# Moving the second half of the agent input from VectorE to ScalarE in a recurrent kernel, and one state sum ahead of the first cell's terms

## The reference, cut to what matters

```python
encoded = tanh(xt @ We + st @ Ue + be)
new_state = tanh(einsum('bd,cds->bcs', xt, Wx) + einsum('bs,cst->bct', st, Ws) + bk)
mem = concatenate([concatenate([encoded, err[:, None]], 1)[:, None, :], mem[:, :-1, :]], 1)
a = relu(mem.reshape(b, -1) @ enc_w1 + enc_b1)
agent_in = relu(a @ enc_w2 + enc_b2)
h1, c1 = lstm_cell(agent_in, h1, c1, ...)      # cell 0
h2, c2 = lstm_cell(h1, h2, c2, ...)            # cell 1
gate = softmax(h2 @ gate_w + gate_b)
gate = gate * theta + gs * (1.0 - theta)       # theta from the last 10 errors
st = einsum('bc,bcs->bs', gate, new_state)     # the state: product, then sum over c
pred = clamp01(st[:, -1]); err = pred - yt
```

## Time and profile before

| What | us |
|---|---|
| median of 3 runs | 5460.53 (5460.39 to 5464.48) |
| the profiled execution, its own time | 5460.57 |
| its span in the trace | 5458.7 |
| TensorE matmuls busy | 5391.8 |
| VectorE busy | 4479.8 |
| ScalarE busy | 3807.2 |
| GpSimd busy | 2421.7 |

### The profile page before, as it was taken

How to read it: one execution, slowest core, us unless ns; L and a number is a source line. 1 busy time by engine, 2 the same in 40 slices (tenths; PEclk the granted TensorE clock), 3 DMA queues, 4 the chain that set the end, 5 groups by cost and what they waited for, 6 DMA issues and landing times.

```text
span 5458.7 us, 188210 instructions
## 1 busy us (share of the span) xinstructions
PE 5391.8 (99%) x67584; PEld 3426.0 (63%) x67584; DVE 4479.8 (82%) x12336; ACT 3807.2 (70%) x9729; POOL 2421.7 (44%) x4613
## 2 busy tenths in 40 slices
PE   8999999999999999999999999999999999999998
PEld 5666666666666666666666666666666666666665
DVE  7888888888888888888888888888888888888887
ACT  5777777777767777777777777777777777777775
POOL 3444444444444444444444444444444444444444
PEclk9999999999999999999999999999999999999999
DMA  2111111111111111111111111111111111111111
GB/s 69 29 29 32 29 32 29 32 29 32 29 32 29 32 29 30 31 29 32 29 32 29 32 29 32 29 32 29 30 31 29 32 29 32 29 32 29 32 29 40
DMA packets 299285, 172.38 MB, mean 32 GB/s; under 512 B 156734, under 2 KB 263882, under 8 KB 298714
## 3 DMA queue, kind: packets, MB, share of 16 engines
q1 hardware_dynamic: 293568, 159.42, 11.2%
q10 hardware_dynamic: 5146, 3.66, 0.2%
HBM read 74.65 MB, written 2.10 MB: 14 GB/s over the span
## 4 chain that ended last, share of the span: by engine, by line
PE 95%; DVE 4%; issue 1%; DMA 0%; POOL 0%; ACT 0%; DVEq 0%; ACTq 0%; POOLq 0%
PE a_ps L366 26%; PE chain L417 17%; PE cand_ps L338 9%; PE a_ps L377 9%; PE cand_ps L347 7%; PE chain L310 5%; PE chain L317 4%; PE chain L403 4%; PE chain L293 4%; PE a_ps L388 3%; PE chain L435 3%; PE cand_ps L330 3%; DVE mixed L799 1%; DVE state L817 1%; DVE added L720 1%
## 5 line engine op out<-in xcount | busy, mean ns | idle before, releaser
L366 PE MATMUL a_ps<-hist,w_hist 125*64 125x512 f16 x12288 | 1896.3, 383 | 24.1 <-DMA w_hist<-enc_table 24.1
L817 DVE TENSOR_REDUCE state<-mixed 128x64 f32<-128x512 f32 x2048 | 1353.4, 682 | 34.2 <-POOL mixed L920 0.8
L920 POOL TENSOR_TENSOR mixed<-cand,gate 128x512 f32<-128x512 f32 x1024 | 1281.1, 1272 | 48.6 <-POOL gate L908 12.5
L554 ACT ACTIVATE cand<-cand_ps 128x512 f32<-128x512 f32 x2048 | 1101.8, 593 | 91.1 <-PE cand_ps L347 90.6
L417 PE MATMUL chain<-cell_in,cell_w 128*64 128x128 f32 x16384 | 1120.7, 278 | 19.8 <-DVE cell_in L735 19.8
L886 POOL TENSOR_TENSOR one_theta<-ones,theta 128x8 f32<-128x8 f32 x512 | 103.4, 202 | 2241.0 <-DVE theta L702 2241.0
L417 PEld LDWEIGHTS chain<-cell_in,cell_w 128*64 128x64 f32 x16384 | 889.2, 136 | 271.5 <-DVE cell_in L735 211.8
L366 PEld LDWEIGHTS a_ps<-hist,w_hist 125*64 125x64 f16 x12288 | 681.4, 109 | 536.2 <-issue 141.7
L561 ACT ACTIVATE gates<-chain 128x384 f32<-128x384 f32 x1024 | 502.0, 490 | 726.3 <-PE chain L417 726.1
L735 DVE SCALAR_TENSOR_TENSOR cell_in<-gates,tanh_c 64x128 f32<-64x128 f32 x2048 | 582.5, 284 | 127.0 <-ACT tanh_c L571 113.4
L720 DVE SCALAR_TENSOR_TENSOR added<-gates 128x256 f32<-128x256 f32 x1024 | 537.1, 524 | 141.2 <-ACT gates L561 141.2
(11 more groups left out here) (76 smaller groups left out, 6823.8 us busy)
## 6 DMA issues: line engine op xcount, KB each, us to landing
x_sb<-in_x_l SPq DMA_DIRECT2D x260, 256.0 KB, 2.7
hist<-entry_parts SPq DMA_DIRECT2D x2048, 25.0 KB
w_hist<-enc_table SPq DMA_DIRECT2D x258, 128.0 KB, 2.4
y_rows<-in_y_l SPq DMA_DIRECT2D x260, 8.0 KB
ys<-in_y ACTq DMA_DIRECT2D x1, 2048.0 KB, 16.3
preds_out<-preds SPq DMA_DIRECT2D x1, 2048.0 KB, 7.5
cand<-in_encoder ACTq DMA_DIRECT2D x1, 640.0 KB, 3.8
cell_w<-in_cell ACTq DMA_DIRECT2D x2, 256.0 KB, 4.5
```

The costliest lines, as they stand in the source:

```text
L366: nc.tensor.matmul(a_ps[g][ENC * half:ENC * half + ENC, :], w_hist[0:HROWS, w_slot(u), kk, wp, :], hist[0:HROWS, xp, k, at:at + 512], star ...
L554: ins = nc.scalar.activation(cand[:, g, q // 2, :, q % 2, :, :].rearrange("p h s c -> p h (s c)"), cand_ps[q][:, :].rearrange("p (h k) -> ...
L817: V.tensor_reduce(state[:, g, hf, 2 * pair:2 * pair + 2, :], mixed[:, pair, hf, :, :, :], AX, ALU.add)\
L920: G.tensor_tensor(mixed[:, 0, :, q, :, :], cand[:, g, 0, :, q, :, :], over_s, ALU.mult)\
```

## The change

ScalarE does both halves of the agent input, one after the other, and only the second raises `q_in`. VectorE's `agent_input` and the semaphore `q_in_high` go. On VectorE the product `mix(old, 1)` follows the gate directly, and the sum (1, 1) moves from after the sum (1, 0) to ahead of `cell_terms(cur, 0)`.

```diff
@@ TensorE, cell_gates
                 if c == 0:
                     pe.wait_ge(q_in, n)
-                    pe.wait_ge(q_in_high, n)
                     pe.wait_ge(q_hnext, n)
@@ ScalarE, agent_input
-                nc.scalar.activation(cell_in[0][rows, g, hf, :], a_ps[g][rows, 0:P], ACT.Relu,
-                                     bias=enc2_bias[rows, 0:1]).then_inc(q_in, 1)
+                last = nc.scalar.activation(cell_in[0][rows, g, hf, :], a_ps[g][rows, 0:P], ACT.Relu,
+                                            bias=enc2_bias[rows, 0:1])
+                if hf == HF - 1:
+                    last.then_inc(q_in, 1)
@@ ScalarE, phase
                 if new:
                     agent_input(new, 0)
+                    agent_input(new, 1)
                     cell_tanhs(new, 0)
@@ VectorE, agent_input removed
-            def agent_input(item, hf):
-                g, n, u = item
-                rows = AGENT_ROWS[hf]
-                dve.wait_ge(q_inps, n)
-                V.tensor_scalar(cell_in[0][rows, g, hf, :], a_ps[g][rows, 0:P], enc2_bias[rows, 0:1], 0.0,
-                                ALU.add, ALU.max).then_inc(q_in_high, 1)
@@ VectorE, phase
                 if old:
                     fresh_gate(old)
                     new_gate(old)
-                if cur:
-                    agent_input(cur, 1)
-                if old:
                     mix(old, 1)
                     mix_sum(old, 0, 1)
+                    mix_sum(old, 1, 1)
                 if cur:
                     cell_terms(cur, 0)
                     cell_value(cur, 0)
@@
                 if old:
                     mix_sum(old, 1, 0)
-                    mix_sum(old, 1, 1)
```

More of the change, by code:

```diff
@@ L150, in recurrent_kernel @@
         q_out_gate = [sem(f"q_out_gate{c}") for c in range(2)]
-        q_in_high = sem("q_in_high")
         q_sum = [[sem(f"q_sum{hf}_{pair}") for pair in range(2)] for hf in range(HF)]
```

## The result

The changed kernel takes 5559.93 us (5559.83 to 5564.15, 4 runs) against 5460.46 us before (median of 4 runs), a ratio of 1.0183 with a 95% interval of 1.0165 to 1.0201. It is slower by 99.5 us; the forecast was 5590, slower by 129.5, with a range of 5520 to 5621. The profiled execution took 5564.15 us, its span is 5562.3.

The account below looks back on a forecast made before the run. TensorE's list bounds the kernel, with no slack at the agent input. ScalarE's second half costs 0.26 or 0.30 us per ordinary phase, nothing where a turn begins: 127.5 us over 51 turns, 5588, called 5590; range 5520 to 5621.

Parts of the forecast that it names:

- first rival: ScalarE's two agent-input activations overlap by 0.11 us, so L417 is only 0.22 us late: 68 us slower, 5529; chance 0.23.
- likeliest case: ScalarE's two activations do not overlap, first cell group 0.35 us later: 5590, spanning 5575 to 5615; chance 0.66.
- The agent input has no slack; 0.35 us later.: At TensorE's first L417, inputs and TensorE come within 0.05 us of each other; ScalarE's second half delays it 0.35 us.
- No overlap of the two activations.: On ScalarE the second half starts after the first with a gap of 0.02 us, 0.38 after its start.
- the nearest row: ScalarE's traced pair L579 then L566, one beginning at partition 64, gap 0.02 us, taken as model for the new pair.
- VectorE's two moves cancel.: On VectorE, L799 0.61 us earlier offsets the moved sum's 0.60, leaving the queue free for L720 at 3024.79, as before.
- GpSimd holds L720; nothing is lost where a turn begins.: L720 ends 0.28 us after GpSimd's product; in the turn's first phase TensorE's 0.35 fits its 0.58 wait, costing nothing.
- 0.05 to 0.09 us given back at the second cell group.: TensorE's wait for VectorE's hidden state at the second L417 vanishes, leaving net 0.30 or 0.26 us an ordinary phase.
- the touch at the transposes: Last sum and TensorE's transposes touch at the phase's end; slack there worth at most 0.05 us, counted as no gain.

Follow-up runs that it names:

- the run without bias: Changed kernel with the bias left out of both ScalarE halves of the agent input: 5476.91 us (ratio 1.0029 to the kernel before).
- The run with VectorE's list kept: Kernel before with both agent-input halves on ScalarE; in L744's place VectorE runs a spare instruction reading PSUM, same wait and signal: 5563.20 us (1.0190).

## Why the prediction was right, and where its size was off

The time alone would not have told the forecast from its first rival. 5560 lies 30 us below 5590 and 31 above the 5529 of overlapping activations. It is inside the range, which was wide enough to take in both, but outside the 5575 to 5615 of the likeliest case. The traces decide: the two activations are 0.38 apart and the first cell group is 0.35 late. With the give-back at its measured size, an estimate is 5567 for the forecast's case (459 x 0.23 us) and 5506 for the overlap (459 x (0.22 - 0.12) us, with the 0.12 that the run without bias gave back).

- **The agent input has no slack; 0.35 us later.** Right: 0.35 us. The run with VectorE's list kept (5563) shows that this alone makes the time.
- **No overlap of the two activations.** Right: 0.38 apart. The choice of the nearest row decided between 5590 and 5529. The reason given for it, that both instructions must begin at partition 0, was only half right: 64 then 64 overlaps as well. For this pair both readings give the same, which was luck. The Trainium skill (ScalarE: Activation LUTs, What ACT_TABLE_LOAD costs) has back-to-back activations overlap by about 93 ns; here it holds where both begin at the same partition (0.25 to 0.27 apart for 0.35 to 0.36 long), and not for the pair of the change.
- **VectorE's two moves cancel.** Right: L721 comes from the queue in time and waits 0.21 us for ScalarE. The sum alone costs 190 us, the sum with the earlier product nothing.
- **GpSimd holds L720; nothing is lost where a turn begins.** Right: 11.02 to 11.04 us, and cutting GpSimd's product gives the kernel before 88 us.
- **0.05 to 0.09 us given back at the second cell group.** This is the mis-sized term of the sum: 0.07 in the mean of the nine ordinary phases, where 0.12 was given back. The prediction took off only the wait from start to start. In the mean over the ordinary phases, TensorE's starts in both traces give: first cell group +0.350; L403 to the second group -0.063 (the wait counted); second group to the next L366 -0.051 (0.924 before, 0.873 after); transposes to the next L366 -0.022; small ones +0.02. That is +0.23. A group that had to wait starts slowly as well: from its start to the next L366 it takes 0.05 us longer where it waited (0.924, in all phases of the kernel before and in the turn's first phase of the changed one) than where it had not (0.873, in the ordinary phases of the changed kernel and of the runs without that wait). The prediction had put the touch at the transposes at "at most 0.05" and then at nothing.
- So the sum would have been 459 x 0.23 = 106 us instead of 127.5. The stretch from the first encoder2 to the last grew by 105.8 us; what lies ahead of it and behind it is 2.3 us shorter, which gives the 103.6 of the spans. The profiled execution was 4.2 us above the three others of its kernel, which leaves the 99.5 of the medians.

The other steps of the forecast's text held in the trace: L799 0.26 after L788, L721 at its free 0.42 us, the first cell group 3028.64 - 3027.85 = 0.79 after the first activation.

## What to carry to other kernels

Where two engines do the halves of a step side by side and the result is awaited at once, merging them on one engine makes the result later by the whole second half, however idle that engine is (0.35 us here), and only waits further on give part of it back (0.12 us here). The slots freed on the other engine pay only if its queue is the bound. An instruction whose duration grows with nothing else changed (0.42, 0.55, 1.08 us for L720) may be held inside by another engine, and what ends just before it each time says by which. Take what a wait is worth from the length of the group with and without the wait, not only from the gap ahead of it. And price a loop's first phase by itself, with each of its late engines.

## What the runs showed of the hardware that was not expected

- Two activations back to back on ScalarE overlap by about 0.1 us where both begin at the same partition (0 then 0, 64 then 64) and not where the start partition changes (0.36 to 0.38 apart for 0.35 to 0.36 long).
- A `tensor_scalar` on VectorE from SBUF to SBUF, 64x128 in fp32, took 1.23 or 1.26 us when it started while GpSimd's product ran, 0.28 us when it had ended before that product began, and 0.34 us with a PSUM source beside the product. It ended 0.10 us after the first of two products that follow each other, while L720 in the earlier trace rows starts in the second and ends 0.28 after it. In every phase of the kernel before that L720 ends 0.28 us after GpSimd's second product (510 phases, none over 0.01 from it), whatever its start. The products on VectorE with one input in PSUM (L799) kept their 1.20 to 1.22 us beside GpSimd.
- After a wait TensorE's group of 16 matmul instructions takes 0.05 us longer than without one. The records show the first pair 0.16 us ahead of the next, and all other pairs 0.11.
